# Conditioned adapter on one core: the last down sum moves behind batch 1's last-quarter units, and half of batch 3 is stored as whole rows

## What is computed

```python
def _L0_cond_ref(x, h_lang, Wd, bd, Wu, bu, Wdd, bdd, Wdu, bdu):
    dWd = ((h_lang @ Wdd.T + bdd) * DELTA_SCALE).reshape(B, BN, D)
    dWu = ((h_lang @ Wdu.T + bdu) * DELTA_SCALE).reshape(B, D, BN)
    Wd_b = Wd + dWd
    Wu_b = Wu + dWu
    down = jax.nn.relu(jnp.einsum('bld,bnd->bln', x, Wd_b) + bd)
    up = jnp.einsum('bln,bdn->bld', down, Wu_b) + bu
    return x + up
```

## Time and profile before

| | us |
|---|---|
| median of 3 runs (211.11 to 211.42) | 211.13 |
| time of the profiled execution | 211.07 |
| its span, first to last instruction | 209.3 |
| PE busy, share of the span | 170.2 (81%) |
| DVE busy | 158.7 (76%) |
| POOL busy | 76.6 (37%) |
| ACT busy | 58.5 (28%) |
| DMA: mean rate over the span | 407 GB/s |

### The profile page before, as it was taken

One profiled execution on the slowest core, in us unless ns is written; L12 is line 12 of the kernel. 1 busy time (PEld: TensorE's weight loads), 2 busy tenths in 40 slices (PEclk: granted clock), 3 DMA queues, 4 the chain that ended last, 5 costly groups with the idle time before them and its releaser, 6 DMA issues.

```text
span 209.3 us, 3113 instructions
## 1 busy us (share of the span) xinstructions
PE 170.2 (81%) x1172; PEld 101.7 (49%) x1172; DVE 158.7 (76%) x87; ACT 58.5 (28%) x106; POOL 76.6 (37%) x61
## 2 busy tenths in 40 slices
PE   1066598865699485899999989999988999998970
PEld 0011151422174022376876748668745656657960
DVE  2868996999999999944854967458879999974470
ACT  2000023112011202043554435445532454534000
POOL 2000000000000000026857827988465789899000
PEclk9999996889659969699999999999999999999997
DMA  6999999999999999999999999999999999999998
GB/s 228 421 413 421 424 423 420 420 423 421 421 423 421 426 420 423 418 424 421 420 423 421 418 418 420 418 424 421 423 415 423 415 418 416 422 383 386 347 343 281
DMA packets 19544, 85.11 MB, mean 407 GB/s; under 512 B 1478, under 2 KB 9675, under 8 KB 10444
## 3 DMA queue, kind: packets, MB, share of 16 engines
q1 hardware_dynamic: 19520, 84.94, 99.9%
q10 hardware_dynamic: 12, 0.00, 0.0%
HBM read 76.55 MB, written 8.39 MB: 406 GB/s over the span
## 4 chain that ended last, share of the span: by engine, by line
DMA 57%; PE 21%; DVE 16%; issue 2%; SPq 0%; DVEq 0%
DMA w<-in_L_cond_Wdd_dram 30%; DMA w<-in_L_cond_Wdu_dram 27%; DVE wt L316 15%; PE bank L672 12%; PE acc L554 5%; PE dn L648 2%; PE acc L682 1%; PE gt L580 1%; PE bank L637 0%; SPq L243 0%; DVE xs L359 0%; DVE down L348 0%; DVEq L358 0%
## 5 line engine op out<-in xcount | busy, mean ns | idle before, releaser
L316 DVE STREAM_TRANSPOSE wt<-w 128x2048 f32<-128x2048 f32 x63 | 145.5, 2311 | 33.0 <-DMA w<-in_L_cond_Wdu_dram 23.8
L554 PE MATMUL acc<-wt,st 128*32 128x512 f32 x496 | 73.4, 720 | 28.4 <-DVE wt L316 28.4
L501 POOL TENSOR_TENSOR xs<-xs,bu_all 128x1024 f32<-128x1024 f32 x16 | 37.9, 2369 | 101.2 <-PE bank L637 101.1
L554 PEld LDWEIGHTS acc<-wt,st 128*32 128x32 f32 x496 | 14.7, 123 | 66.7 <-issue 34.0
L672 PE MATMUL bank<-wu_b,down 128*128 128x128 f32 (+1 forms) x216 | 31.5, 298 | 0.5 <-issue 0.5
L672 PEld LDWEIGHTS bank<-wu_b,down 128*128 128x128 f32 x216 | 27.9, 191 | 7.5 <-issue 5.7
L648 PE MATMUL dn<-xt,wd_b 128*128 128x256 f32 x128 | 30.6, 382 | 0.0
L508 POOL TENSOR_TENSOR xs<-up_s,xs 128x512 f32<-128x512 f32 (+1 forms) x23 | 27.8, 1232 | 7.5 <-ACT up_s L452 7.5
L648 PEld LDWEIGHTS dn<-xt,wd_b 128*128 128x128 f32 x128 | 23.0, 190 | 4.3 <-issue 1.8
L392 ACT ACTIVATE g_rows<-acc 128x512 f32<-128x512 f32 x16 | 9.6, 598 | 42.4 <-PE acc L554 40.9
L434 ACT ACTIVATE xt<-bank 128x512 f32<-128x512 f32 x32 | 17.4, 597 | 8.4 <-PE bank L637 8.4
(11 more groups left out here) (35 smaller groups left out, 36.2 us busy)
## 6 DMA issues: line engine op xcount, KB each, us to landing
w<-in_L_cond_Wdd_dram SPq DMA_DIRECT2D x32, 1024.0 KB, 7.4
w<-in_L_cond_Wdu_dram SPq DMA_DIRECT2D x32, 1024.0 KB, 10.1
xs<-in_x_dram SPq DMA_DIRECT2D x7, 1024.0 KB, 12.2
out_dram<-xs SPq DMA_DIRECT2D x3, 1024.0 KB, 11.9
out_dram<-xs SPq DMA_DIRECT2D x6, 512.0 KB, 4.4
out_dram<-xs SPq DMA_DIRECT2D x5, 256.0 KB, 4.4
xs<-in_x_dram SPq DMA_DIRECT2D x2, 512.0 KB, 9.7
out_dram<-xs SPq DMA_DIRECT2D x1, 768.0 KB, 9.5
```

The lines of the kernel that those rows point to most:

```text
L316: nc.vector.transpose(wt[:, tslot].rearrange("p r (k j) -> p k r j", j=QUAD), w[:, slot, :].rearrange("p (k r h) -> p k r h", r=R, h=QUAD) ...
L501: nc.gpsimd.tensor_tensor(xs[:, b, i0:i0 + UNIT_I], xs[:, b, i0:i0 + UNIT_I], bu_pair, ALU.add).then_inc(bu_added, 1)
L554: last = nc.tensor.matmul(a[TILE * place:TILE * (place + 1)], st[:, r, low * TILE:(low + 1) * TILE], wt[:, slot + h, r], start=low == 0 an ...
```

## The change

The units of the last quarter and the last down sum change places, and the stores of batch 3 are cut another way.

- Unit (3, 0, 4, 256, 128), the third quarter of rows 0 to 3 of batch 3, is dropped as a unit of its own, and so is (3, 0, 4, 384, 128). Two units of two rows and 256 columns, (3, 0, 2, 256, 256) and (3, 2, 2, 256, 256), take their place at the very end. There are 34 units before and after. POOL has 22 of them, not 23.
- Ahead of the last pair of sums stands one unit (2, 0, 4, 256, 128) where three stood. The two small third-quarter units of batch 2 go behind the turn of the last group.
- The last down sum goes behind both last-quarter units of batch 1. Before it stood behind (0, 4, 4, 384, 128).
- Store 3 takes rows 0 to 3 of batch 3 only (512 KB). Rows 4 to 7 of batch 3 are stored once, over the whole of D, as one store of 1 MB (new store 11). The pieces of rows 0 to 3 in the second half of D follow as new stores 12 and 13. There are 14 stores, not 15.

```diff
-UNITS += [(2, 0, 4, 2 * QD, QD), (2, 4, 2, 2 * QD, QD), (2, 6, 2, 2 * QD, QD), (3, 0, 4, 2 * QD, QD)]
+UNITS += [(2, 0, 4, 2 * QD, QD), (2, 4, 2, 2 * QD, QD), (2, 6, 2, 2 * QD, QD)]
 UNITS += [(0, 0, 2, 3 * QD, QD), (0, 2, 2, 3 * QD, QD), (0, 4, 4, 3 * QD, QD)]
-UNITS += [(b, i, 4, 3 * QD, QD) for b in range(1, B) for i in range(0, I, 4)][:-1]
+UNITS += [(b, i, 4, 3 * QD, QD) for b in range(1, B - 1) for i in range(0, I, 4)]
 UNITS += [(B - 1, I - 4, 2, HALF, HALF), (B - 1, I - 2, 2, 0, HALF), (B - 1, I - 2, 2, HALF, HALF)]
+UNITS += [(B - 1, i, 2, HALF, HALF) for i in range(0, I - 4, 2)]
...
-POOL_UNITS = 23
+POOL_UNITS = 22
...
-UP_COUNT = {8: 1, 9: 1, 14: 2, 16: 1, 19: 2, 20: 2, 21: 1, 22: 2, 23: 1, 24: 2, 25: 1, 26: 1, 27: 2, 28: 2}
+UP_COUNT = {8: 1, 9: 1, 14: 2, 16: 1, 19: 2, 20: 2, 21: 1, 22: 2, 23: 1, 24: 2, 25: 1, 26: 1, 27: 2, 28: 1}
...
-UP_BEFORE_SUM = UP_BEFORE_LAST + 1
-UP_BEFORE_DOWN = UP_BEFORE_SUM + 4
+UP_BEFORE_SUM = UP_BEFORE_LAST
+UP_BEFORE_DOWN = UP_BEFORE_SUM + 7
...
-STORES = [(b, slice(0, I), slice(0, HALF)) for b in range(B - 1)] + [(B - 1, slice(0, I - 2), slice(0, HALF))]
+STORES = [(b, slice(0, I), slice(0, HALF)) for b in range(B - 1)] + [(B - 1, slice(0, 4), slice(0, HALF))]
 STORES += [(0, slice(i, i + 2), slice(HALF, D)) for i in range(0, 4, 2)] + [(0, slice(4, I), slice(HALF, D))]
-STORES += [(b, slice(i, i + 4), slice(HALF, D)) for b in range(1, B) for i in range(0, I, 4)][:-1]
-STORES += [(B - 1, slice(I - 2, I), slice(0, HALF))]
-STORES += [(B - 1, slice(i, i + 2), slice(HALF, D)) for i in range(I - 4, I, 2)]
+STORES += [(b, slice(i, i + 4), slice(HALF, D)) for b in range(1, B - 1) for i in range(0, I, 4)]
+STORES += [(B - 1, slice(4, I), slice(0, D))]
+STORES += [(B - 1, slice(i, i + 2), slice(HALF, D)) for i in range(0, 4, 2)]
```

More of the change, by code:

```diff
@@ L92 @@
     BANK_USE += [("up", e) for e in UP_AT.get(_t, ())]
-BANK_USE += [("up", e) for e in range(UP_BEFORE_LAST, UP_BEFORE_SUM)]
 BANK_USE += [("x", 2 * LAST_DOWN), ("x", 2 * LAST_DOWN + 1)]
@@ L476, in _ @@
                     copy_up(e)
-            for e in range(UP_BEFORE_LAST, UP_BEFORE_SUM):
-                copy_up(e)
             copy_group(2 * GROUPS - 1, 1)
@@ L531, in _ @@
                     finish_unit(e)
-            for e in range(UP_BEFORE_LAST, UP_BEFORE_SUM):
-                finish_unit(e)
             add_bu(LAST_DOWN)
@@ L662, in up_unit @@
                 b, rows, cols = unit_at(e)
-                if e == 0 or cols.stop > unit_at(e - 1)[2].stop:
+                if cols.stop > max([unit_at(before)[2].stop for before in range(e)], default=0):
                     pe.wait_ge(group_added, min(cols.stop * GROUPS // D, GROUPS - 1))
@@ L705, in _ @@
                     up_unit(e)
-            for e in range(UP_BEFORE_LAST, UP_BEFORE_SUM):
-                up_unit(e)
             for a in range(LAST_PARTS):
```

## The result

The changed kernel takes 210.25 us (median of 6 runs, 210.0 to 210.96) against 211.33 us of the kernel before (6 runs, 211.11 to 211.6). The ratio is 0.9957, 95% interval 0.9943 to 0.9972: 0.9 us of 211 (0.6 to 1.2 us by the interval). The forecast was 0.59 us.

The account below looks back on a forecast made before the run. The prediction took the queue of stores, its bytes' readiness and rate, as the bound. Savings of 0.47 (run length), 0.12 (hole) and 0 (PE order) sum to 0.59 us off 211.07 us: 210.5 us, range 209.9 to 211.2 us.

Parts of the forecast that it names:

- the run length: Stores of batch 3: 1 MB in 8 KB instead of 1 KB runs moves at 421 GB/s, saving 0.47 us.
- the order on PE: Units in the tail: stores 4 to 6 ready 0.6 us earlier, PE's later end covered by the store queue, cost 0.
- the hole: DMA stretch near 196 us, short of work at 252 GB/s: bounds 0 and 0.24 us, half taken, saving 0.12 us.
- The bound: End of the kernel: set by the queue of stores; engines matter only if a store becomes ready after the queue empties.
- The rival: New 1 MB store: late rate not set by run length, 378 GB/s, saves 0.19 us, time 210.9 us; chance 0.22.
- The whole queue speeds up: Late stores: earlier readiness returns the 1 KB runs to 384 GB/s, 1.08 us more, time 209.5 us; chance 0.10.
- The timeline: Tail: store 11 ready at 202.0 us, PE ending at 202.9 us, DVE's last sum at 203.7 us.
- the margin of 0.6 to 0.9 us: Ahead of store 11: its packets can start 0.9 us before they are needed, or 0.6 us by the upper bound.
- The slower rival: Between stores 10 and 11: the queue runs empty ahead of the 1 MB store, gap 1.1 us, time 211.6 us; chance 0.10.
- The rule against it: 1 MB store: smaller DMAs may start sooner, the change does the opposite; by this rule a gap opens ahead of store 11.

Follow-up runs that it names:

- half rows: Changed kernel with rows 4 to 7 of batch 3 stored as two halves of D in 1 KB runs: 210.6 us, ratio 0.9975 to the kernel before.
- down sum only: Kernel before with only the last down sum moved, behind the first last-quarter unit of batch 1: 210.7 us, ratio 0.9977.
- down sum back: Changed kernel with the last down sum put back between the two last-quarter units of batch 1: 210.3 us, ratio 0.9953 to the kernel before.
- early stores small: Changed kernel with stores 0 to 2 each cut into two stores of four rows: 210.3 us, ratio 0.9959 to the kernel before.
- two whole stores: Changed kernel with the 1 MB store split into rows 4 and 5, then 6 and 7, in 4 KB runs: 210.42 us, ratio 0.9955 to the kernel before.
- stores only: Kernel before with its order of units kept and only the stores changed, the 1 MB store last: 211.38 us, ratio 1.0011.
- all whole: Changed kernel without store 3, all of batch 3 stored as whole rows: 211.4 us, ratio 1.0016 to the kernel before.
- hole made: Changed kernel with store 4 held until unit 24 is done: 212.25 us, ratio 1.0039 to the kernel before.
- held: Changed kernel with stores 4 to 13 held until DVE has finished its last unit: 224.23 us (1 run).
- merged: Changed kernel with the second halves of batches 1 and 2 stored as one 1 MB store each: 210.93 us, ratio 0.9983 to the kernel before.

## Why the prediction was right, and where it was off

The two terms came out as 0.34 us for the run length (forecast 0.47) and 0.49 us for the order on PE with the hole (forecast 0.12). The first was put 0.13 us too high and the second 0.37 us too low. The two errors partly cancel, so that the sum is off by only 0.3 us is in part luck.

**The bound.** Right. The tail is the queue of stores, and what the units cost on PE showed only through the time at which a store was ready.

**The run length.** Right in mechanism. The 1 MB moved at 420 GB/s, as taken (421), and not at 378 or 345. Forecast 0.47 us; half rows less changed kernel is (0.9975 - 0.9959) x 211 = 0.34 us. The rival's figure for the new store (378 GB/s) falls. What it started from does not: late stores in 1 KB runs stay slower than early ones with the same runs, in every version.

**The order on PE.** This is the term that was mis-sized. I asked only what a later end of PE costs, priced that at 0, and gave the hole 0.12 us (at most 0.24), because I put the hole down to the issue of store 6. Measured is 0.49 us for the place of the down sum alone. The second profile of the kernel before shows my error: the hole belongs to store 7, which stood behind the last down sum, and I had its readiness in my list (195.0 us, while the earlier trace rows show it issued at 197.36 us before) without asking what that was worth to the kernel before. Of the 0.49 us, 0.24 us are the hole. For the rest the late stretch gives a number: 198.5 to 203.5 us moved at 342 GB/s before and at 358 in the kernel with only the down sum moved (these are one trace each), which over 5 us is 5 x (1 - 342/358) = 0.22 us. The split is not firm: against the second profile of the kernel before (367, 300 and 349 GB/s in the three windows, where the kernel with only the down sum moved has 373, 380 and 358) the same sums give 0.35 us ahead of 198.5 us and 0.13 us behind it. The window of the kernel before:

```profile
198.50:203.50 5.00, 4.15 (x26) 3.49 (x25) 4.03 (x6) 0.00 (x0) 0.00 (x0) 1.00 1.03 342
```

**The whole queue speeds up.** I gave this rival 0.10 and 1.08 us, back to 384 GB/s. A small part of it may be real. Counting only up to the first packet of whole rows, seven traces without a hole ahead of the stretch from 198.5 us move its 1 KB packets at 352 to 364 GB/s (changed kernel 355 and 361, half rows 363, down sum only 358, down sum back 352 with a short hole in the stretch itself, early stores small and two whole stores 364). Six with a hole or a standstill ahead have 337 to 349 (before 342 and 349, stores only 340, all whole 338, hole made 337, held 339). The merged kernel fits only in part, with 367 behind its shallow hole and 350 behind its deep one. No trace goes back to 384. That stores are ready earlier, as I wrote, is not enough for it: held back and all ready they got 339.

**The timeline.** Shifted by 0.85 us, store 11 was issued at 202.2 us (forecast 202.0), DVE ended at 203.8 us (203.7), PE at 203.0 us (202.9). The queue did not run empty ahead of store 11: it was issued at 203.02 us, and at 204.3 us its packets move at the full rate. But the margin of 0.6 to 0.9 us that I gave it was not there, since the stores ahead of it moved faster than the 345 GB/s that I took: its first packet came just as the queue began to run out, in the second trace with 12 to 13 packets in flight for 0.2 us instead of 16. Two whole stores, with the first issued 1.8 us earlier, gained nothing, so this cost nothing that shows. The slower rival did not come, but the kernel with all of batch 3 whole shows its mechanism and its price.

**The rule against it.** By the Trainium skill, "Perfetto Trace Analysis", section "DMA Optimizations", splitting DMAs into smaller chunks may let some of them start sooner. The merged kernel bears it out for this place (0.5 us lost by merging, through two holes), even with DMA engines that are busy elsewhere all the time. Splitting the whole rows in two gained nothing.

**Open.** Why late stores in 1 KB runs are slower than early ones is not settled, and neither is whether a hole adds to it. The size and the cut of the stores are excluded. The traces with a hole ahead are slower by 3 to 27 GB/s, but that is one trace each (two of the kernel before and of the changed one), and from 203.5 us on the kernel with half rows, which had no hole, is down to 349 GB/s as well. The one run meant to make a hole made two. No late stretch had its stores issued as far ahead of their turn as the early ones. Nor is it settled why single issues take 1.5 to 1.8 us.

## What to carry to other kernels

Where the tail is a queue of stores, list for each store when it is ready and when the queue reaches it; a unit of work moved on an engine that "is covered" is worth the hole that it fills, and here perhaps somewhat more (0.24 to 0.35 us of the 0.49 are the hole). Long contiguous runs pay (420 instead of 349 GB/s in the same place here), but only if the bytes taken out of earlier stores are not the ones that bridged the queue. And profile the kernel before twice: a stall that wanders can put a hole in another place than its cause.

## What was not expected of the hardware

- The last 0.9 us of DMA work has a share of 0.61 to 0.66 in the changed kernel and in that with half rows, and 0.89 in the kernel before. The second row is the kernel with only the down sum moved:

```profile
207.50:208.40 0.90, 0.00 (x0) 0.00 (x0) 0.00 (x0) 0.00 (x0) 0.00 (x0) 0.50 0.89 313
206.95:207.85 0.90, 0.00 (x0) 0.00 (x0) 0.00 (x0) 0.00 (x0) 0.00 (x0) 0.50 0.86 303
```

  That a hole in the queue brings the engines into step again would fit the first of these, but not the second: that kernel had no hole and finishes almost as evenly as the kernel before. The cause is open.
- The issue of one store takes 0.37 us, but in seven of the fourteen traces one of them near 195 to 197 us takes 1.5 to 1.8 us (1.48, 1.73 and 1.81 us above). In the changed kernel one 16 KB packet of the instruction queue falls into 196.0 to 197.8 us, the stretch of that issue:

```profile
q8 instruction: 1, 0.02, 3.2%
```

  In each of the seven the long issue starts within 0.4 us of the start of such a packet. But in two others (down sum only, stores only) an issue that starts 0.1 and 0.3 us after such a packet takes 0.37 us, so this is a coincidence in time and no proof.
